# A Macaron transformer block on one core: a separate instruction order for the first attention group of the first batch

## What is computed

```python
xqkv = x @ Wqkv                      # 16 query heads, 4 key/value heads of 128
xq, xk = apply_rotary_emb(xq), apply_rotary_emb(xk)
scores = einsum('bqhd,bkhd->bhqk', xq, xk) * scale + causal_add
probs = softmax(scores)
attn = einsum('bhqk,bkhd->bqhd', probs, xv)
return attn @ Wo
...
x = x + 0.5 * ffn(layernorm(x))
x = x + attn(layernorm(x))
x = x + 0.5 * ffn(layernorm(x))
```

## Time and profile before

| what | value |
|---|---|
| median of three runs | 847.01 us (845.07 to 847.35) |
| time of the profiled execution | 845.92 us |
| its span | 844.1 us |
| TensorE busy | 764.2 us (91%) |
| VectorE, ScalarE, GpSimd busy | 651.8, 581.1, 450.5 us |
| granted TensorE clock, mean | 0.975 |

### The profile page before, as it was taken

How to read it: one execution, slowest core, us unless ns; L and a number is a source line. 1 busy time by engine, 2 the same in 40 slices (tenths; PEclk the granted TensorE clock), 3 DMA queues, 4 the chain that set the end, 5 groups by cost and what they waited for, 6 DMA issues and landing times.

```text
span 844.1 us, 16346 instructions
## 1 busy us (share of the span) xinstructions
PE 764.2 (91%) x4584; PEld 657.9 (78%) x4584; DVE 651.8 (77%) x1884; ACT 581.1 (69%) x1534; POOL 450.5 (53%) x398
## 2 busy tenths in 40 slices
PE   3698999799999999999999999999999789999980
PEld 3586887687878888888888887888887678797970
DVE  6675665578898878889988989987889978756572
ACT  2365667787877888877878778788777566555650
POOL 1571605587556685575657556454454685004274
PEclk8799999999999999999999999999999999999995
DMA  9598962121000100010010000000000055356785
GB/s 305 147 348 256 286 180 76 63 32 20 1 2 13 20 14 8 1 17 10 2 14 13 2 1 2 1 2 1 7 1 1 26 207 162 110 162 207 212 246 179
DMA packets 53206, 70.90 MB, mean 84 GB/s; under 512 B 7296, under 2 KB 44928, under 8 KB 52736
## 3 DMA queue, kind: packets, MB, share of 16 engines
q1 hardware_dynamic: 41024, 47.80, 18.2%
q0 software_dynamic: 9216, 16.82, 8.1%
q10 hardware_dynamic: 2880, 5.24, 1.9%
HBM read 42.80 MB, written 27.03 MB: 83 GB/s over the span
## 4 chain that ended last, share of the span: by engine, by line
PE 62%; DVE 12%; POOL 11%; issue 7%; DMA 3%; ACT 2%; DVEq 0%; SPq 0%; POOLq 0%; ACTq 0%
PE ps L1749 51%; PE ps L1954 6%; POOL sb_ropeB L1695 2%; POOL sb_xf L1698 2%; PE ps L1807 2%; DVE sb_x L1521 1%; POOL xs L1656 1%; DMA sb_wF_raw<-ys,sb_pos 1%; POOL sb_x L1686 1%; POOL xs L1664 1%; POOL sb_wF L1706 1%; DVE sb_prob L1494 1%; PE ps L1821 1%; DVE sb_wF L1501 1%; PE ps L1915 1%
## 5 line engine op out<-in xcount | busy, mean ns | idle before, releaser
L1749 PE MATMUL ps<-sb_wF 128*128 128x512 f32 (+2 forms) x1056 | 261.2, 374 | 7.5 <-DVE sb_wF L1511 5.0
L1749 PEld LDWEIGHTS ps<-sb_wF 128*128 128x128 f32 x1056 | 172.7, 190 | 26.9 <-issue 5.5
L1042 ACT ACTIVATE sb_prob<-sb_prob,sb_nmax 128x128 f32<-128x128 f32 (+3 forms) x256 | 142.2, 559 | 39.7 <-DVE sb_nmax L1494 38.9
L1695 POOL TENSOR_TENSOR sb_ropeB<-sb_ropeB,sb_sin 128x512 f32<-128x512 f32 x80 | 111.0, 1388 | 104.1 <-ACT sb_ropeB L1023 104.0
L1749 PE MATMUL ps<-sb_wF,sb_wA 128*128 128x512 f32 x576 | 154.9, 404 | 6.0 <-ACT sb_ropeB L1023 5.2
L1706 POOL TENSOR_TENSOR sb_wF<-sb_xf,sb_wF 128x384 fp32r<-128x384 f32 (+1 forms) x75 | 82.2, 1104 | 119.3 <-ACT sb_wF L1035 119.1
L1521 DVE SCALAR_TENSOR_TENSOR sb_x<-ps,sb_rinv,sb_x 128x256 f32<-128x256 f32 x256 | 122.6, 479 | 20.4 <-PE ps L1749 9.2
L1749 PEld LDWEIGHTS ps<-sb_wF,sb_wA 128*128 128x128 f32 x576 | 102.1, 188 | 32.0 <-ACT sb_ropeB L1023 13.3
L1051 ACT ACTIVATE sb_wF<-ps 128x512 fp32r<-128x512 f32 x160 | 95.4, 596 | 42.8 <-PE ps L1954 42.0
L1501 DVE TENSOR_TENSOR sb_wF<-ps,sb_wF 128x512 fp32r<-128x512 f32 x160 | 109.3, 684 | 19.4 <-ACT sb_wF L1051 18.1
L1749 PE MATMUL ps<-sb_wA,sb_wF 128*128 128x256 f32 x768 | 115.4, 286 | 7.6 <-DVE sb_x L1521 4.9
(11 more groups left out here) (198 smaller groups left out, 1284.4 us busy)
## 6 DMA issues: line engine op xcount, KB each, us to landing
ys<-sb_wA_raw SPq DMA_DIRECT2D x124, 128.0 KB, 2.5
sb_wF_raw<-xs SPq DMA_DIRECT2D x44, 128.5 KB, 3.9
sb_wA_raw<-xs SPq DMA_DIRECT2D x44, 128.5 KB, 2.8
sb_work<-xs SPq DMA_DIRECT2D x36, 128.5 KB, 2.9
sb_wA_raw<-in_wattn ACTq DMA_DIRECT2D x18, 256.0 KB, 5.0
sb_wF_raw<-in_wgu SPq DMA_DIRECT2D x4, 768.0 KB, 10.3
sb_wF_raw<-in_wdn SPq DMA_DIRECT2D x4, 768.0 KB, 12.7
sb_wA_raw<-in_wgu SPq DMA_DIRECT2D x4, 768.0 KB, 7.2
```

The costliest lines, as they stand in the source:

```text
L1042: nc.scalar.activation(own, own, ACT.Exp, scale=-1.0, bias=nmax[:, k % 2, h:h + 1], accum_out=ssum[:, k % 2, h:h + 1]).then_inc(exp_done, 1)
L1695: nc.gpsimd.tensor_tensor(ropeB[:, slot], ropeB[:, slot], sin[:], ALU.mult).then_inc(rope_mul, 1)
L1749: return nc.tensor.matmul(out, lhsT, rhs, start=start, stop=stop)
```

## The change

The change gives the first group of the first batch lists of its own, `ORDER_FIRST`. `head_of` takes them in place of the common `ORDER`. GpSimd's list is the same as before. VectorE's step for the first projection (`Jd,0,4`) is put ahead of the evacuation of the last expert tile, through `BESIDE`. No instruction is added or taken away; the same ones stand in another order on three engines. Of the new lists TensorE's is shown whole.

```diff
+    ORDER_FIRST = {
+        "pe": """
+        S,0,0 S,0,1 J,0,4 S,0,2 S,0,3 S,1,0 S,1,1 T,0,0 J,0,0 S,1,2 S,1,3 S,2,0 V,0,0 J,0,1 T,1,0 S,2,1 S,2,2 T,1,1
+        W,0,0 J,0,2 V,1,0 S,2,3 W,0,1 V,1,1 S,3,0 J,0,3 T,2,0 T,2,1 S,3,1 J,0,5 S,3,2 V,2,0 J,0,6 S,3,3 T,2,2 W,1,0
+        V,2,1""",
+        "act": """
...
+        "pool": """
+        PM,0,4 PL,0,4 PM,0,0 PL,0,0 PM,0,1 PL,0,1 PM,0,2 PM,0,3 PL,0,2 PL,0,3""",
+    }
...
-    BESIDE = {"pe": {-1: [("S", 0, 0), ("S", 0, 1)], 0: [("J", 0, 4)]}, "dve": {0: [("max", 0, 0), ("max", 0, 1)]}}
+    BESIDE = {"pe": {-1: [("S", 0, 0), ("S", 0, 1)], 0: [("J", 0, 4)]}, "dve": {0: [("max", 0, 0), ("max", 0, 1), ("Jd", 0, 4)]}}
 
     def head_of(engine):
         ahead = [item for items in BESIDE.get(engine, {}).values() for item in items]
-        return [item for item in group_order(engine, 0) if item[1] >= 0 and item not in ahead]
+        return [item for item in group_order(engine, 0, ORDER_FIRST) if item not in ahead]
```

More of the change, by code:

```diff
@@ L317, in program @@
     }
+    ORDER_FIRST = {
[4 more added lines that the diff above has]
+        "act": """
+        exp,0,0 exp,0,1 Ja,0,4 exp,0,2 exp,0,3 exp,1,0 exp,1,1 Ja,0,0 pt_hi,0,0 rope_hi,0,4 exp,1,2 exp,1,3 Ja,0,1
+        a_hi,0,0 rope_hi,0,0 pt_hi,1,0 exp,2,0 exp,2,1 pt_hi,1,1 Ja,0,2 exp,2,2 rope_hi,0,1 exp,2,3 a_hi,1,0 exp,3,0
+        Ja,0,3 pt_hi,2,0 rope_hi,0,2 pt_hi,2,1 Ja,0,5 exp,3,1 exp,3,2 Ja,0,6 pt_hi,2,2 exp,3,3 rope_hi,0,3""",
+        "dve": """
+        max,0,0 max,0,1 Jd,0,4 max,0,2 max,0,3 max,1,0 max,1,1 Jd,0,0 recip,0,0 pt_lo,0,0 max,1,2 max,1,3 max,2,0
+        Jd,0,1 a_lo,0,0 pt_lo,1,0 max,2,1 max,2,2 recip,1,0 pt_lo,1,1 Jd,0,2 x_add,0,0 x_add2,0,0 max,2,3 x_add,0,1
+        x_add2,0,1 a_lo,1,0 max,3,0 Jd,0,3 recip,2,0 pt_lo,2,0 pt_lo,2,1 max,3,1 max,3,2 Jd,0,6 max,3,3 x_add,1,0""",
+        "pool": """
+        PM,0,4 PL,0,4 PM,0,0 PL,0,0 PM,0,1 PL,0,1 PM,0,2 PM,0,3 PL,0,2 PL,0,3""",
+    }
     def group_order(engine, g, table=None, first=False):
```

## The result

The changed kernel took 854.93 us (median of four runs, 853.8 to 856.63), the kernel before 846.69 us (four runs, 845.07 to 847.35). The ratio is 1.0097, with a 95% interval from 1.008 to 1.0115: 8.2 us slower. The forecast was 852.5 us with a range from 848.6 to 855.2.

A forecast was written before the change was run, and what follows sets the result against it. The prediction took TensorE, with 62% of the last chain, as the bound. It added +4.9 us for the order and +0.6 for the clock, +5.5 on the median 847.01, giving 852.5 us, range 848.6 to 855.2.

The forecast's parts named there:

- the walk: Step-by-step pass through the first group's new lists with profiled durations; it put the order's cost at +4.9 us.
- the last T: Last transposes of the first group, said to wait for exp,3,3 and be out at 187.1: +4.9 us.
- V,0,0 waited: V,0,0 ahead of J,0,1: TensorE waits 2.1 us because pt_hi,0,0 is queued behind Ja,0,0; J,0,1 +1.1.
- W,0,1's x_adds: W,0,1 ahead of J,0,3 waits for two x_adds behind Jd,0,2 on VectorE; J,0,3 +4.3 us.
- The wait at W,0,0: W,0,0 ahead of J,0,2: about 1.8 us, with a_hi,0,0 behind Ja,0,1; J,0,2 +2.2.
- The route of exp,3,3: Group's end: exp,3,3 late through GpSimd, then ScalarE's copies and Jd,0,6 ahead of max,3,3; ends at 186.8.
- swallowed: Rival: waits in the next groups absorb lateness, 4.9 shrinks to about 1.6 us, time 848.6; chance 0.07.
- GpSimd had slack: At the next group GpSimd is free at 190.3, so the key's PM still waits for Ja (193.2).
- The early Jd: Jd,0,4 ahead of the last evacuation starts 0.85 us sooner; gain spent at once, as T,0,0 precedes J,0,0.
- The granted clock: TensorE falling to 1.2 GHz after long waits: 1.4 us at most per fall, one chance in two, 0.6 added.
- the forecast's own range: Range around the main forecast of 852.5 us: 850 to 854.5, given a chance of 0.72.
- the wide one: Range for 8 in 10: 848.6 us (lateness absorbed) to 855.2 us (two clock falls).
- The rival of two falls: Rival: the clock falls more than once in the first group, about +8 us, time 855; chance 0.12.

The follow-up runs named there:

- e12: Changed kernel plus unused identity transposes on TensorE in the waits at V,0,0, W,0,0 and W,0,1: 852.12 us against 847.78 for the kernel before, ratio 1.0051.
- e9: Changed kernel measured once more, not edited: 853.44 us against 847.45 for the kernel before, ratio 1.0065.
- e10: Changed kernel with max,3,3 put ahead of Jd,0,6 on VectorE: 851.72 us against 847.45 for the kernel before, ratio 1.0045.
- e11: Changed kernel with the first two x_adds put ahead of Jd,0,2 on VectorE: 853.27 us, ratio 1.008 to the kernel before.
- e5: Changed kernel with pt_hi,0,0 put ahead of Ja,0,0 on ScalarE: 850.64 us, ratio 1.0039 to the kernel before.
- e6: Changed kernel with V,0,0 put back behind J,0,1 on TensorE: 852.14 us, ratio 1.0064 to the kernel before.
- e2: Kernel before with only VectorE's Jd,0,4 put ahead of the last expert tile's evacuation: 846.65 us against 847.38, ratio 0.9985.

## Why the prediction was right, and which term was too small

The starts of the steps after J,0,4, in us; the walk's shifts are those of the prediction:

| step | before | walk | e12, full clock | after, one fall | e9, two falls |
|---|---|---|---|---|---|
| J,0,0 | 4.54 | +0.1 | +0.18 | +0.18 | +0.20 |
| J,0,1 | 9.36 | +1.1 | +1.23 | +1.29 | +1.56 |
| J,0,2 | 14.08 | +2.2 | +2.30 | +3.59 | +3.87 |
| J,0,3 | 18.69 | +4.3 | +4.65 | +5.93 | +7.10 |
| J,0,5 | 22.84 | +4.3 | +4.12 | +5.40 | +7.28 |
| J,0,6's transposes | 26.40 | +3.6 | +3.47 | +4.73 | +6.57 |
| next group's first J | 32.40 | +4.9 | +4.49 | +5.80 | +7.22 |

(The walk's last shift is that of the last T, one step ahead.)

- **The steps.** Each step of the walk is met within 0.41 us where the clock stays up. V,0,0 waited 2.20 (forecast 2.1), W,0,1's x_adds stood behind Jd,0,2, which started at 177.39, 1.0 after J,0,2 was done, and the last T waited for exp,3,3. The wait at W,0,0 was 1.21 to 1.51 us (after, e9, e10, e11), under the forecast 1.8. Three causes are confirmed by taking each away: Ja ahead of pt_hi (e5), Jd,0,2 ahead of the x_adds (e11), Jd,0,6 ahead of max,3,3 (e10). e6 shows that the waits at W don't come from V's place.
- **The route of exp,3,3.** The walk had it late through GpSimd. The trace has little of that: rope_hi,0,2 waited 0.34 us for GpSimd (at 186.30), in e9 not at all. e10 shows that the place of Jd,0,6 was enough for the wait. The size of this step came out right, its route in part.
- **Shift kept to the end.** Nothing was swallowed: +5.80 at the next group's first J, and without the 5.28 from the experts +5.82 at 251.07 and +5.68 at 676.83. With them every step stood some 11 us later, and not 5 to 6, in this profile. The key's PM of the next group waited 2.89 us for its Ja, where it had been 1.62, so GpSimd had slack, as the walk said.
- **The early Jd** gave 0.83 by itself (e2, forecast 0.85), and none in the changed kernel, since T,0,0 stood ahead of J,0,0.
- **The granted clock** is the term that was too small. I took 0.6 us: one fall for the whole group, at one chance in two, less what is hidden. Measured are 1.31 us (after, one fall) and 2.73 (e9, two). Among the profiles of this group there are twelve waits of 2.02 to 2.41 us, and 1.2 GHz followed ten of them; it stayed up behind 2.04 (after) and 2.19 (e11). The changed kernel has two such waits in each execution. At 1.31 to 1.37 each, 2 x 10/12 gives 2.2 to 2.3 us. With e12's 4.49 that is 6.7 to 6.8, and the two measurements have 8.2 and 6.0, 7.1 in the mean. By these runs each of the long waits had to be priced, and not the group once. The rate is that of this group and not a rule, as the last batch shows below. The Trainium skill ("TensorE: Matmul & The Clock Gate", section "What's actually happening") says that an idle array is put to 1.2 GHz. Ten cases of twelve agree, where the earlier trace rows had one of two.
- **Where luck comes in.** 854.93 lies above the forecast's own range (850 to 854.5) and 0.3 us inside the wide one; the second measurement, 853.44, lies in both. The rival of two falls had 0.12 and the number nearest to the first median, 855. But the profile of that measurement has one fall and not two, and its J,0,4 is late from the experts, so the number was met by luck. Two falls are what e9 shows. Two profiles can't tell how often each case comes.
- **What stays open.** Why the first measurement was 2.2 us above the second is not settled. The profiles put J,0,4 anywhere between 151.6 and 157.15, in the one looked at (after) with waits for loads and a fall of the clock in the experts, and the two sets of four and six runs overlap (853.8 to 856.63, 852.21 to 856.37).
